# Decoder layer on one core: attention values in column tiles, the residual added in PSUM, layer norm applied on ScalarE, and the output product moved behind the next scores

## What is computed

```
x = layernorm(x + attn(x))                 # causal self-attention, W1 b1, W2 b2
x = layernorm(x + xattn(x, ctx, ctx))      # window of 64 behind, 64-token blocks
h = x + attention(rms_norm(x, w1))         # rope, grouped keys and values, no biases
h = h + moe(rms_norm(h, w2))               # router, top 2 of 8, three products each
out = layernorm(x + h)
```

```
q, k, v = x @ Wq + bq, k_in @ Wk + bk, k_in @ Wv + bv   # per head: 8 features
w = softmax(mask(q @ k.T / sqrt(8)))                    # 64 x 64 per head
out = concat_heads(w @ v) @ Wo + bo
layernorm(y) = (y - mean(y)) / sqrt(var(y) + 1e-5)      # over the 128 features
```

## Time and profile before

| | us |
|---|---|
| median of 3 runs | 279.54 (279.23 to 280.69) |
| the profiled execution, its own time | 280.07 |
| its span in the trace | 278.3 |
| granted clock of TensorE, mean over the span | 0.891 |
| scores of step 0 start (L541) | 16.11 |
| last `xm` of step 23 starts (L948) | 158.47 |
| TensorE busy | 216.4 (78%) |
| VectorE busy | 190.3 (68%) |
| ScalarE busy | 119.1 (43%) |
| GpSimd busy | 115.6 (42%) |

### The profile page before, as it was taken

How to read it: one execution, slowest core, us unless ns; L and a number is a source line. 1 busy time by engine, 2 the same in 40 slices (tenths; PEclk the granted TensorE clock), 3 DMA queues, 4 the chain that set the end, 5 groups by cost and what they waited for, 6 DMA issues and landing times.

```text
span 278.3 us, 6021 instructions
## 1 busy us (share of the span) xinstructions
PE 216.4 (78%) x1736; PEld 193.7 (70%) x1737; DVE 190.3 (68%) x510; ACT 119.1 (43%) x393; POOL 115.6 (42%) x204
## 2 busy tenths in 40 slices
PE   0489999999999999989999653199999999930000
PEld 0368899899989988879988552089999999920000
DVE  7135799888799999997785349546766767633534
ACT  1437667566756664557734211043344344400000
POOL 0243235443566666653311420444454432017771
PEclk9999999999999999999999555589999999985555
DMA  7899800000005200000000000011211233012112
GB/s 233 169 349 355 196 4 0 0 2 4 2 2 149 80 0 4 1 0 12 12 19 21 14 7 0 19 39 41 57 47 47 47 47 38 19 38 57 47 47 75
DMA packets 21334, 16.00 MB, mean 57 GB/s; under 512 B 3032, under 2 KB 18464, under 8 KB 21312
## 3 DMA queue, kind: packets, MB, share of 16 engines
q1 hardware_dynamic: 19248, 12.02, 15.1%
q0 software_dynamic: 1344, 2.76, 4.9%
q10 hardware_dynamic: 720, 0.95, 1.1%
HBM read 11.78 MB, written 3.93 MB: 56 GB/s over the span
## 4 chain that ended last, share of the span: by engine, by line
PE 61%; DVE 16%; issue 7%; POOL 7%; DMA 5%; ACT 2%; SPq 2%; POOLq 0%; DVEq 0%; ACTq 0%
PE bank L677 12%; PE bank L571 11%; PE bank L493 9%; PE bank L688 8%; PE bank L545 6%; POOL yg L482 4%; DVE smax L884 3%; PE bank L581 3%; PE bank L541 2%; DVE x L936 2%; DMA early<-xm_scratch,tok_i 2%; PE bank L588 2%; PE bank L529 2%; DVE s_sb L892 2%; DMA bias_col<-in_L_xattn_bv 2%
## 5 line engine op out<-in xcount | busy, mean ns | idle before, releaser
L571 PE MATMUL bank<-vbd,pt_sb 128*128 128x34 f32 x384 | 46.3, 276 | 0.2 <-ACT pt_sb L767 0.2
L571 PEld LDWEIGHTS bank<-vbd,pt_sb 128*128 128x128 f32 x384 | 44.8, 192 | 0.3 <-ACT pt_sb L767 0.3
L470 POOL DMA_INDIRECT early<-xm_scratch,tok_i x26 | 26.6, 1022 | 44.4 <-DMA early<-xm_scratch,tok_i 26.8
L884 DVE TENSOR_REDUCE smax<-bank 128x8 f32<-128x512 f32 x48 | 32.6, 679 | 13.4 <-PE bank L545 13.4
L677 PE MATMUL bank<-xgt,w_now 128*128 128x128 f32 x320 | 40.3, 281 | 0.4 <-ACT xgt L839 0.4
L677 PEld LDWEIGHTS bank<-xgt,w_now 128*128 128x128 f32 x320 | 38.5, 197 | 0.8 <-ACT xgt L839 0.8
L380 POOL TENSOR_TENSOR k<-kt,cst 128x512 f32<-128x512 f32 x24 | 25.3, 1052 | 33.0 <-ACT kt L757 33.0
L892 DVE TENSOR_TENSOR s_sb<-bank,smax 128x512 f32<-128x512 f32 x48 | 33.2, 692 | 1.9 <-PE bank L493 0.2
L843 ACT ACTIVATE s_sb<-bank,w_now 128x128 f32<-128x128 f32 x80 | 22.8, 368 | 23.8 <-PE bank L677 23.8
L545 PE MATMUL bank<-k,q 64*128 64x256 f32 x192 | 27.6, 400 | 0.0
L767 ACT ACTIVATE pt_sb<-bank 128x512 f32<-128x512 f32 x48 | 26.0, 594 | 3.2 <-PE bank L493 2.7
(11 more groups left out here) (159 smaller groups left out, 347.4 us busy)
## 6 DMA issues: line engine op xcount, KB each, us to landing
w_up<-in_L_ffn_W SPq DMA_DIRECT2D x2, 2048.0 KB, 12.5
w<-in_L_ffn_W SPq DMA_DIRECT2D x8, 256.0 KB, 6.2
y_scratch<-eo SPq DMA_DIRECT2D x1, 1536.0 KB, 6.9
y_scratch<-eo SPq DMA_DIRECT2D x10, 128.0 KB
cst<-in_consts ACTq DMA_DIRECT2D x1, 672.5 KB, 4.3
early<-in_x SPq DMA_DIRECT2D x1, 512.0 KB, 6.1
early<-in_ctx SPq DMA_DIRECT2D x1, 512.0 KB, 4.4
xm_scratch<-xm SPq DMA_DIRECT2D x8, 64.0 KB, 1.5
```

Source lines behind the costliest of these rows:

```text
L470: pool.indirect_dma_start(xg[:, j, :], None, xm_d[:, :], bass.IndirectOffsetOnAxis(ap=tok_i[:, j:j + 1], axis=0)).then_inc(g_gather, 16)
L571: k = mm(ps_o[:, c:c + 34], pt_sb[:, h, (2 * b + jj) * P:(2 * b + jj + 1) * P], vbd[:, i, b, j, :, :].rearrange("k p c -> k (p c)"), start ...
L884: v.tensor_reduce(smax[:, b, :], ps_score[b][:, :].rearrange("q (p k) -> q p k", k=S), AX.X, ALU.max).then_inc(d_mx, 1)
```

## The change

The product of exponentials and values is turned round. Now v is what is loaded into the array, in column tiles: four products write the four groups of 32 partitions of `ps_o`, each with 32 weight columns, and the exponentials stream through. There are 8 products of 128 columns for the row sums (weights `ones_d`, so that every feature row gets its head's sum) and 16 of 64 columns for the values. The result is already turned, so `turn_o`, `copy_ot` and `o_sb` go. `norm_o` becomes one reciprocal of 128 x 128 and one multiplication of 128 x 128 that writes `ot_sb`. The value bias is no longer added in `copy_ot`; `value_bias` and `fold_value_bias` multiply it by the output weights once and add it to the residual's bias row. `first_residual` waits for that.

The residual is added by TensorE: `out_proj` starts with a product of `ident` with `res_b` into the same 128 columns of `ps_y`. The statistics are read from `ps_y` directly, and so is the normalised tile: `finish` is now one ScalarE instruction that reads `ps_y` with a scale and a bias for each row, for which `row_scale` makes a fifth column (minus mean times scale). `ps_y` has one buffer, so `out_proj(n)` waits on `a_x` for `finish(n - 1)`.

The order changes: `out_proj(it - 2)` stands right behind `scores(it)`. On VectorE `add_res(it - 2)` is last in the turn, behind the maxima of `it`. On GpSimd `row_scale(it - 2)` of the first two stages follows `expand_keys(it + 2)`, `rotate(it - 3)` and `add_bias(it - 3)`. On ScalarE `finish(it - 3)` is first in the turn. The rope copies of the second stage and `xm` stay on VectorE (`rope`, `pre_norm`).

The core of the diff; removed bodies that stand in the listing above are left out:

```diff
-        vbd = sb("vbd", [P, 4, 2, 4, 2, 17])
+        vbd = sb("vbd", [P, 4, 2, 4, 80])
+        ones_d = sb("ones_d", [P, 2, 32])
-        rsum = sb("rsum", [P, 2, 2 * NP])
-        o_sb = sb("o_sb", [P, 2, 2, NP, 2, HD])
+        rsum = sb("rsum", [P, 2, P])
...
-        res = sb("res", [P, 2, D])
...
                 pool.wait_ge(in_x, 16)
-                pool.wait_ge(in_w3rd, 16 * 9)
+                pool.wait_ge(d_vb, 2)
...
+                        pool.wait_ge(a_x, n - 1)
                         if n - 2 >= NT:
                             pool.wait_ge(d_ra, 2 * (n - 2 - NT + 1))
                     g.tensor_scalar(r[:, 0:1], mv[:, i, 1:2], LN_EPS, None, ALU.add).then_inc(g_rq, 1)
                     link()
-                    g.tensor_tensor(r[:, 1:2], r[:, 0:1], half_neg[:, :], ALU.pow).then_inc(g_rs, 1)
+                    g.tensor_tensor(r[:, 1:2], r[:, 0:1], half_neg[:, :], ALU.pow).then_inc(g_rq, 1)
+                    link()
+                    g.tensor_scalar(r[:, 4:5], mv[:, i, 0:1], r[:, 1:2], -1.0, ALU.mult, ALU.mult).then_inc(g_rs, 1)
...
-                if it >= 3:
+                if it - 3 >= 2 * NT:
                     row_scale(it - 3)
                 if it + 2 < STEPS:
                     expand_keys(it + 2)
                 rotate(it - 3)
-                if it >= 4:
-                    add_bias(it - 4)
+                if it >= 3:
+                    add_bias(it - 3)
+                if 0 <= it - 2 < 2 * NT:
+                    row_scale(it - 2)
...
+            def values(n):
+                i = n % 4
+                pe.wait_ge(a_pt, 2 * n + 2)
+                pe.wait_ge(a_v, 4 * (n + 1))
+                if n >= 1:
+                    pe.wait_ge(d_o, n)
+                for a in range(2):
+                    for j in range(4):
+                        h, jj = j // 2, j % 2
+                        p = pt_sb[:, h, :].rearrange("k (b j a q) -> k b j a q", b=2, j=2, a=2)
+                        mm(ps_o[32 * j:32 * j + 32, P:2 * P], ones_d[:, a, :], p[:, :, jj, a, :],
+                           start=(a == 0), stop=(a == 1))
                 for b in range(2):
...
+                    for a in range(2):
+                        for j in range(4):
+                            h, jj = j // 2, j % 2
+                            c = (2 * b + jj) * P + a * S
+                            k = mm(ps_o[32 * j:32 * j + 32, b * S:(b + 1) * S], vbd[:, i, b, j, a * 32:(a + 1) * 32],
+                                   pt_sb[:, h, c:c + S], start=(a == 0), stop=(a == 1))
                 k.then_inc(pe_o, 1)
 
...
+            def out_proj(n):
+                s, t, i = n // NT, n % NT, n % 2
+                if n == 0:
+                    pe.wait_ge(d_vb, 2)
                 if n >= 1:
...
+                    pe.wait_ge(a_x, min(n, 2 * NT))
+                if n >= 2 * NT + 1:
+                    pe.wait_ge(d_res, t)
+                if s < 2:
+                    pe.wait_ge(c_resb, 1 if s == 0 else t + 2)
+                    mm(ps_y[:, 0:P], ident, res_b[:, s, t, :], start=True, stop=False)
+                pe.wait_ge(d_o, n + 1)
+                mm(ps_y[:, 0:P], ot_sb[:, i, :], w_o[:, s, :], start=(s == 2), stop=True).then_inc(pe_y, 1)
+            def value_bias():
+                pe.wait_ge(in_b, 96)
+                pe.wait_ge(in_w, 32)
+                for s in range(2):
+                    k = mm(ps_y[:, s * P:(s + 1) * P], bias_col[:, s, 2:3].to_broadcast([P, P]), w_o[:, s, :],
+                           start=True, stop=True)
+                k.then_inc(pe_vb, 1)
...
+            value_bias()
             pe.wait_ge(c_bf, 2)
             for it in range(STEPS + 2):
                 if it < STEPS:
                     scores(it)
+                if 2 <= it:
+                    out_proj(it - 2)
                 if it + 2 < STEPS:
                     turn_x(it + 2)
                 if 1 <= it <= STEPS:
...
                     turn_p(it - 1, 1)
                 if it + 2 < STEPS:
                     project(it + 2)
-                if 2 <= it:
-                    turn_o(it - 2)
                 if 1 <= it <= STEPS:
-                    values(it - 1, 0)
-                    values(it - 1, 1)
-                if 2 <= it:
-                    out_proj(it - 2)
+                    values(it - 1)
...
+                if n >= 1:
+                    act.wait_ge(pe_o, n)
...
+                        k = A(vbd[p2 * S:(p2 + 1) * S, i, b, :, :]
+                              .rearrange("k j (a c) -> k j a c", a=2)[:, :, :, p2 * 16:p2 * 16 + HD],
+                              ps_v[b * S:(b + 1) * S, :]
+                              .rearrange("k (j p a d) -> k j p a d", p=2, a=2, d=HD)[:, :, p2, :, :], ACT.Copy)
+                        k.then_inc(a_v, 1)
+            def finish(n):
+                s, t, i = n // NT, n % NT, n % 2
+                act.wait_ge(g_rs, cnt_rs(n) - s)
+                A((x1, x2)[s][:, t, :], ps_y[:, 0:P], ACT.Identity, bias=rstd[:, i, 4:5],
+                  scale=rstd[:, i, 1:2]).then_inc(a_x, 1)
...
+                if 3 <= it < 2 * NT + 3:
+                    finish(it - 3)
...
+                dve.wait_ge(pe_o, n + 1)
                 if n >= 2:
...
+                    dve.wait_ge(d_o, n - 1)
+                v.reciprocal(rsum[:, i, :], ps_o[:, P:2 * P]).then_inc(d_rs, 1)
                 dve.wait_ge(d_rs, n + 1)
                 if n >= 2:
...
+                    dve.wait_ge(pe_y, n - 1)
+                v.tensor_tensor(ot_sb[:, i, :], ps_o[:, 0:P], rsum[:, i, :], ALU.mult).then_inc(d_o, 1)
+            def fold_value_bias():
+                dve.wait_ge(pe_vb, 1)
+                dve.wait_ge(in_w3rd, 16 * 9)
+                for s in range(2):
+                    v.tensor_tensor(bias_row[:, s, :], ps_y[:, s * P:(s + 1) * P], bias_row[:, s, :],
+                                    ALU.add).then_inc(d_vb, 1)
...
             def add_res(n):
                 s, t, i = n // NT, n % NT, n % 2
                 dve.wait_ge(pe_y, n + 1)
                 if s < 2:
...
+                    v.bn_stats(stats[:, i, :], ps_y[:, 0:P]).then_inc(d_st, 1)
                     dve.wait_ge(d_st, n + 1)
                     if n >= 2:
                         dve.wait_ge(g_rs, cnt_rs(n - 2))
                     v.bn_aggr(mv[:, i, :], stats[:, i, :]).then_inc(d_mv, 1)
                 else:
...
+                    dve.wait_ge(a_x, NT + t + 1)
+                    v.tensor_tensor(h3[:, t, :], ps_y[:, 0:P], x2[:, t, :], ALU.add).then_inc(d_res, 1)
+            def rope(n):
+                t, i = n - NT, n % 2
+                if 0 <= t < NT:
+                    dve.wait_ge(a_x, n + 1)
+                    dve.wait_ge(g_rs, cnt_rs(n))
...
+            def pre_norm(n):
+                t, i = n - 2 * NT, n % 2
+                if t >= 0:
+                    dve.wait_ge(g_rs, cnt_rs(n))
...
             for it in range(STEPS + 3):
                 if 2 <= it < STEPS + 2:
                     norm_o(it - 2)
-                if it >= 3:
-                    add_res(it - 3)
                 if it < STEPS:
                     row_max(it, 0)
                     minus_max(it, 0)
                     row_max(it, 1)
                     minus_max(it, 1)
-                if it >= 3:
-                    finish(it - 3)
+                if it == 0:
+                    fold_value_bias()
+                rope(it - 3)
+                pre_norm(it - 3)
+                if 2 <= it < STEPS + 2:
+                    add_res(it - 2)
```

More of the change, by code:

```diff
@@ L573, in values @@
                 k.then_inc(pe_o, 1)
-            def turn_o(n):
-                i = n % 2
-                pe.wait_ge(d_o, 2 * (n + 1))
+            def out_proj(n):
+                s, t, i = n // NT, n % NT, n % 2
+                if n == 0:
+                    pe.wait_ge(d_vb, 2)
                 if n >= 1:
[L579 to L588, removed]
+                    pe.wait_ge(a_x, min(n, 2 * NT))
[4 more added lines that the diff above has]
+                    mm(ps_y[:, 0:P], ident, res_b[:, s, t, :], start=True, stop=False)
@@ L773, in copy_v @@
                 if n == 0:
-                    act.wait_ge(c_zero, 6)
+                    act.wait_ge(c_zero, 8)
                 if n >= 4:
-                    act.wait_ge(pe_o, 2 * (n - 3))
+                    act.wait_ge(pe_o, n - 3)
                 for b in range(2):
                     for p2 in range(2):
-                        A(vbd[p2 * S:(p2 + 1) * S, i, b, :, p2, 0:16],
-                          ps_v[b * S:(b + 1) * S, :]
-                          .rearrange("k (j p c) -> k j p c", p=2, c=16)[:, :, p2, :], ACT.Copy).then_inc(a_v, 1)
-            def copy_ot(n):
-                s = n // NT
-                act.wait_ge(pe_ot, n + 1)
-                if n >= 2:
-                    act.wait_ge(pe_y, n - 1)
-                A(ot_sb[:, n % 2, :], ps_y[:, 0:P], ACT.Identity, bias=bias_col[:, s, 2:3]).then_inc(a_ot, 1)
```

(25 more changed lines are left out.)

55 lines of the change are left out of this document (15 added, 40 removed).

## The result

The changed kernel takes 292.62 us (median of 4 runs, 291.74 to 293.61) against 280.08 (4 runs, 279.23 to 280.69) for the kernel before: a ratio of 1.045, with a 95% interval of 1.040 to 1.050. I had forecast 285.1 (281 to 290). The direction is as forecast; the loss is 12.5 us and not 5.6, and the time lies outside the range. Two of the eleven executions of experiment 1, the profiled one among them, ran at a lower granted clock (0.882) and took 286 us; its ratio leaves them out.

A forecast was written before the change was run, and what follows sets the result against it. A loop of waits through single-buffered ps_y was to set the step. Fifteen steps +8.1, scores 19 to 20 -2.1, third stage -0.7, start +0.85, first steps -0.8, tail +0.1, stated total +5.6: 279.54 becomes 285.1 us, range 281 to 290.

The forecast's parts named there:

- The mechanism: A circle of waits through single-buffered ps_y sets the first two stages' steps; TensorE idles 1.2 us before the residual product.
- The rival that TensorE's own work decides: First stage: GpSimd's part is short enough to hide the loop, 15 steps of 5.1 us, total 269.5 us; chance 0.10.
- the second stage's loop sum of 6.22: Second stage: the ps_y loop through VectorE, rotate, row_scale and finish takes 6.22 us, 6.33 with two turns; counted as 6.25.
- From `rope_a` to `rope_b`: Second-stage loop on VectorE: the first of the two rope copies takes 0.27 us.
- From the residual product to VectorE's subtraction: Second-stage loop: products, input turn and first turn_p take 1.16 us, plus 0.04 for the wait.
- First stage: 6.03 forecast: First stage: the ps_y loop through GpSimd's keys takes 5.92 or 6.03 us, counted as 6.0 a step.
- Third stage: 5.33 for 5.1: Third stage: the step runs through values, reciprocal, multiplication, output product, turns and project, 5.1 us.
- the 1.35 I counted: TensorE: the 48 passes of values take 1.25 us plus 0.1 for the change of tile shape.
- The reciprocal: VectorE: 128 columns take 1.0 us instead of 0.255 for 16, and do not bind in the loop.
- the wait of 7.22 that goes at scores 20: Scores 19 to 20: the 7.22 us step, where TensorE waits 1.06 for a copy behind square, becomes 5.1, -2.1.
- The forecast of TensorE's own work: TensorE's own work in a step falls to 4.7 us, 0.85 less than before.
- the rival in which the tiles take turns: TensorE: column tiles run one after another, values takes 3.45 + 0.1 us, total about 314 us; chance 0.08.

The follow-up runs named there:

- experiment 1: Changed kernel with row_scale(it - 2) first in GpSimd's turn, ahead of expand_keys, rotate and add_bias: 282.37 us, ratio 1.006.
- Experiment 3: Changed kernel with row_scale(it - 2) first on GpSimd and add_res(it - 2) behind VectorE's first row maximum: 265.59 us, ratio 0.951.
- experiment 5: Changed kernel with four unused products (eight passes) added on TensorE ahead of out_proj in 16 turns: 291.56 us, ratio 1.040.
- Experiment 9: The kernel of experiment 4 with rotate(it - 3) ahead of expand_keys(it + 2) on GpSimd: 266.34 us, ratio 0.954.
- experiment 4: Changed kernel's new pieces in the order of the kernel before, only add_bias(it - 3) staying a turn earlier: 271.31 us, ratio 0.968.
- experiment 7: The kernel of Experiment 3 with ScalarE's finish a turn earlier, finish(it - 2) behind copy_qk(it + 2): 265.06 us, ratio 0.946.
- experiment 8: Changed kernel with the reciprocal on 16 of the 128 columns, which changes the output: 287.75 us, ratio 1.024.
- Experiments 2: Changed kernel with add_res(it - 2) right behind the first row maximum on VectorE, not behind all four operations: 292.85 us, ratio 1.046.

## Why the prediction was half right

**The mechanism held.** The range did not: it ended at 290. The loop through the one buffer of `ps_y` is there with every hand-over in the order given, and TensorE idles for ScalarE's `x`, 1.47 us a turn in the first stage and 2.19 in the second for the 1.2 forecast. Experiment 3 removes nothing but two places in that order and takes 27 us off. The rival that TensorE's own work decides is out: steps are 6.2 to 6.9 us, and 0.87 us more work changed nothing (experiment 5). Whether a second buffer of `ps_y` would do the same as the reordering was not tried.

**The step that failed is the second stage's loop sum of 6.22, taken as 6.25 a step.** It measured 6.9, and the seven steps took 49.68 for 43.75, +5.9: some 4.3 from the longer loop and 1.6 from one step at a lower clock. The other misses cancel to +0.3 (+2.0, +0.5 and +0.9 in the first stage, at scores 20 and in the third stage; -1.7, -0.9, -0.4 and -0.1 in the first steps, the tail, the rest and the start), which is luck. So in the trace, 289.9 against a forecast of 283.7, this step is the miss. The medians are 1.3 us further apart (292.62 against 285.1), mostly because the profiled execution before lay 0.5 above the median that I started from, and the one after 0.9 below its own. (My terms as written add up to 5.45; the total said 5.6.) These rows are one turn:
```profile
104.88 0.49 PE L595 MATMUL bank<-early,cst 128*128 128x128 f32 x2 [2.19 <-ACT x L804]
...
106.25 0.69 DVE L908 TENSOR_TENSOR s_sb<-bank,smax 128x512 f32<-128x512 f32 x1 [1.76 <-PE bank L496]
...
107.72 1.05 POOL L379 TENSOR_TENSOR k<-kt,cst 128x512 f32<-128x512 f32 x1 [1.90 <-ACT kt L773]
...
108.18 0.74 DVE L955 SCALAR_TENSOR_TENSOR rope_a<-x,rstd,rope_c 128x128 f32<-128x128 f32 x1
...
108.84 0.34 DVE L955 SCALAR_TENSOR_TENSOR rope_b<-x,rstd,rope_s 128x128 f32<-128x128 f32 x1
...
109.26 0.35 POOL L434 TENSOR_TENSOR xr<-rope_a,rope_b 128x64 f32<-128x64 f32 x1 [0.49 <-DVE rope_b L955]
...
111.27 0.46 ACT L804 ACTIVATE x<-bank,rstd 128x128 f32<-128x128 f32 x1 [2.10 <-POOL rstd L406]
...
111.78 0.49 PE L595 MATMUL bank<-early,cst 128*128 128x128 f32 x2 [2.19 <-ACT x L804]
```
- From `rope_a` to `rope_b` I counted 0.27 and it is 0.66, because the first copy runs beside the expansion of the keys (107.72 to 108.77): +0.39. I had priced the copy from a turn in which nothing ran beside it. Experiment 9 shows the cause, in the order of experiment 4.
- From the residual product to VectorE's subtraction I counted 1.20 with the wait, and it is 1.37: +0.17. 0.1 of it is that the output product starts 0.32 after the residual product, for the 0.22 of two passes. That is not the idle stretch ahead of it: in experiment 7 the distance is 0.33 (62.19 to 62.52) where TensorE does not stand idle. Why it is longer stays open.
- The hand-overs through `rotate`, `row_scale` with its third operation (0.26 for 0.22) and `finish` add 0.12 in all. The sum is 6.22 + 0.39 + 0.17 + 0.12 = 6.90.
- One step of 8.53 instead of 6.9, +1.6. TensorE's clock fell in it, to 0.54 over 89.40 to 92.50, behind a wait of 2.19 us. I had no such term; experiment 5 gave it back by filling the wait.

**Smaller sizes.** First stage: 6.03 forecast, 6.28 measured with two input turns, so +2.0 over eight steps: `k` starts 2.96 after the residual product for 2.82 (0.1 of it again the distance of the two products), `add_bias` to the first `rstd` takes 0.54 for 0.45, and the third `rstd` and the start of `finish` 0.30 for 0.27. Third stage: 5.33 for 5.1. I had sent its step through `values` and `out_proj`; it runs through VectorE's list instead (subtraction, maximum, subtraction, `xm`, `h3`, reciprocal, multiplication, then TensorE's output product and turns, and the subtraction again). In it `xm` (0.75 us at 146.46, beside GpSimd's 1.05 from 146.01) again waits for the expansion, and the reciprocal starts late for that reason. `values` took 1.03 from its first pass to the next scores for the 1.35 I counted; off the loop, that gave nothing back. The first steps saved 2.5 us for 0.8; the loop is not yet closed there, so I take it that TensorE's shorter work counts. The tail saved 0.8 where I had +0.1, but that can't be put down to the change alone: the granted clock was 0.82 over 144 to 158 us before and 1.00 over 157 to 170 us after.

**The terms that were right, or nearly.** The reciprocal (1.0 forecast, 0.94 measured) and its place beside the loop (experiment 8); the start (+0.85 and +0.74); the column tiles, which do not take turns (48 passes in 1.03 us); the wait of 7.22 that goes at scores 20. The forecast of TensorE's own work, 4.7 us a step, is close to experiment 7's 4.79, in whose first stage TensorE is busy 23.66 of 24 us; in part that is luck, as `values` was 0.3 shorter than counted and the two products 0.1 longer.

**What the forecast did not ask.** It stopped at "slower" and took the order as given. Each link of the loop that it lists has a name and a place in an engine's list; two of them, `row_scale` and `add_res`, could be moved, and that was worth 27 us.

## What to carry to other kernels

When a tile in a single buffer is written early in one engine's turn and freed at the end of a chain through three others, write down the whole circle with each engine's order in it, and put the links of the circle ahead of everything that does not belong to it; a single link moved may show nothing while a second loop of about that length stands. Price each link from a row in which the engine beside it does what it will do in the new place. Judge a change's pieces apart from its order: here the column tiles were worth 2.7% by themselves and the order lost 8% (292.6 against 271.3).

## What the hardware showed that I had not expected

**VectorE waits for GpSimd on some operations, and the kernel before shows it already.** The same instruction takes 0.34 or 1.01 us there, timeline of the kernel before, first and second stage:
```profile
58.35 0.34 DVE L936 TENSOR_SCALAR x<-res,mv,rstd 128x128 f32<-128x128 f32 x1
...
121.66 1.05 POOL L380 TENSOR_TENSOR k<-kt,cst 128x512 f32<-128x512 f32 x1
121.78 1.01 DVE L936 TENSOR_SCALAR x<-res,mv,rstd 128x128 f32<-128x128 f32 x1
```
The long one begins behind the start of GpSimd's expansion and ends just after it (122.79 and 122.71). I read its 1.02 us as the price of the operation. After the change `rope_a` (0.74, to 108.92, GpSimd to 108.77), `rope_a` of experiment 4 (1.07) and `xm` (0.75) end 0.14 to 0.15 us behind GpSimd's instruction in the same way, while the subtraction with one operand in PSUM keeps its 0.69 beside it (107.57, beside `k` from 107.72). The Trainium skill (SBUF — State Buffer, "SBUF: two separate sides") says that VectorE, with two inputs in SBUF or in a two-port mode, and GpSimd take a shared pair of ports as a lock for a whole instruction, and whoever comes second is blocked. The trace agrees on who waits, and experiment 9 bears it out. It does not show a wait for the whole instruction: the copies end 0.08 to 0.15 us behind GpSimd's and not their own 0.34.

**TensorE's clock fell behind an idle stretch of 2.19 us, and not each time.** Four later second-stage steps with the same wait of 2.19 us kept the full clock. Experiments 2 and 8 had more of the long steps (8.3 to 8.5 us at a granted clock of 0.80; four and two of them), each with a wait of 2.19 to 2.25 us in it; their steps with waits of 1.13, 1.39 and 1.53 kept the full clock. With the filler, and waits of 1.1 us, there was no fall. What decides between two turns with the same wait stays open.

**Four column tiles over the same rows run at once in float32.** The 16 passes of 128 columns take 0.65 us and the 32 of 64 columns 0.63 (timeline above), with the last pass's own length in each. In turns, the 4096 columns would have taken 3.4 by the 0.84 ns a column of the prediction, an estimate; the rival in which the tiles take turns, and the reading of the rule that stands for it in the prediction, are out.

**The reciprocal costs by its width.** 16 columns take 0.241 us and 128 take 0.939, 6.2 ns for each further column, where VectorE's multiplication of 128 columns takes 0.29.
